# The floor of the sums of squares on VectorE, and GpSimd's root in three pieces with two operations between them

## The reference

```
xn   = layernorm(x)
q, k = l2norm(xn Wq^T), l2norm(xn Wk^T)   # per head, 16 heads of 16; l2norm(t) = t / max(|t|, 1e-6)
v    = xn Wv^T
s    = softmax(q k^T + alibi, window of 128 keys ahead) v, then Wo
h    = silu(fp4(xn) fp4(w_gate)^T) * (fp4(xn) fp4(w_up)^T)
g    = silu(fp4(h) fp4(w_down)^T)
out  = x + s * g
```

## Time and profile before

| | us |
|---|---|
| median of 3 runs | 504.02 (503.54 to 504.03) |
| the profiled execution's own time | 502.66 |
| its span | 500.7 |
| POOL busy | 412.1 (82%), 929 instructions |
| DVE busy | 432.3 (86%), 865 instructions |
| PE busy | 451.3 (90%) |
| ACT busy | 402.2 (80%) |

### The profile page before, as it was taken

How to read it: one execution, slowest core, us unless ns; L and a number is a source line. 1 busy time by engine, 2 the same in 40 slices (tenths; PEclk the granted TensorE clock), 3 DMA queues, 4 the chain that set the end, 5 groups by cost and what they waited for, 6 DMA issues and landing times.

```text
span 500.7 us, 14045 instructions
## 1 busy us (share of the span) xinstructions
PE 451.3 (90%) x4990; PEld 313.9 (63%) x4990; DVE 432.3 (86%) x865; ACT 402.2 (80%) x584; POOL 412.1 (82%) x929
## 2 busy tenths in 40 slices
PE   0467879999999999999999999999999999999997
PEld 0244556666666676676666677667666667666665
DVE  3989988889888888889988988888988888887686
ACT  1466988988888888888887888898888888888952
POOL 6554679999989989899988899989998998988751
PEclk9998999999999999999999999999999999999999
DMA  8211011222222112222221212222222111222200
GB/s 299 90 43 44 12 32 45 65 75 76 75 51 57 38 49 67 65 64 65 65 63 45 63 32 57 65 56 54 54 54 54 44 33 35 54 54 54 45 22 33
DMA packets 78277, 29.35 MB, mean 59 GB/s; under 512 B 67713, under 2 KB 77697, under 8 KB 78209
## 3 DMA queue, kind: packets, MB, share of 16 engines
q1 hardware_dynamic: 77920, 28.39, 22.3%
q10 hardware_dynamic: 288, 0.08, 0.1%
HBM read 7.49 MB, written 4.19 MB: 23 GB/s over the span
## 4 chain that ended last, share of the span: by engine, by line
POOL 56%; issue 17%; PE 5%; DVE 4%; ACT 3%; POOLq 1%; DVEq 0%; ACTq 0%
POOL probs L1514 12%; POOL probs L1507 7%; POOL y L1550 3%; POOL h_q L1544 3%; POOL xq L1526 3%; POOL xn L1604 3%; POOL ss L1562 2%; POOL h_scale L1534 2%; POOL rsq L1582 2%; POOL newton L1586 2%; POOL rsq L1575 2%; POOL x_scale L1521 1%; POOL rsq L1588 1%; POOL newton L1580 1%; POOL newton L1592 1%
## 5 line engine op out<-in xcount | busy, mean ns | idle before, releaser
L1322 ACT ACTIVATE probs<-scores 128x1024 f32<-128x1024 f32 (+1 forms) x101 | 102.3, 1013 | 2.6 <-PE scores L502 1.6
L1507 POOL TENSOR_SCALAR_AFFINE_SELECT probs<-probs 128x512 f32<-128x512 f32 x128 | 81.3, 637 | 1.7 <-ACT probs L1322 1.3
L1514 POOL TENSOR_SCALAR_AFFINE_SELECT probs<-probs 128x512 f32<-128x512 f32 x120 | 76.1, 636 | 3.7
L1200 ACT ACTIVATE qk_stack<-bank_q 128x512 f16<-128x512 f32 x64 | 35.1, 596 | 31.9 <-DVE bank_q L910 31.9
L595 PE MATMUL bank_b<-probs,vals 128*32 128x128 f32 x1952 | 59.7, 274 | 1.1 <-DVE vals L931 0.9
L595 PEld LDWEIGHTS bank_b<-probs,vals 128*32 128x32 f32 x1952 | 52.1, 110 | 7.9 <-DVE vals L931 7.0
L351 PE MATMUL gt<-wgu_hi,xT_hi 128*128 128x352 f16 x128 | 40.3, 315 | 12.1 <-ACT ffn_gate L1336 11.1
L784 DVE SCALAR_TENSOR_TENSOR xT_lo<-gt,xT_hi 128x512 f16<-128x512 f32 (+1 forms) x34 | 22.3, 657 | 27.6 <-ACT xT_hi L1200 27.6
L548 PE MATMUL gt<-wdn_hi,hT_hi 128*128 128x256 f16 x160 | 43.6, 273 | 0.6 <-DVE hT_lo L836 0.6
L548 PE MATMUL gt<-wdn_hi,hT_lo 128*128 128x256 f16 x160 | 43.6, 273 | 0.0
L548 PE MATMUL gt<-wdn_lo,hT_hi 128*128 128x256 f16 x160 | 43.6, 273 | 0.0
(11 more groups left out here) (219 smaller groups left out, 1456.5 us busy)
## 6 DMA issues: line engine op xcount, KB each, us to landing
out<-y SPq DMA_DIRECT2D x32, 128.0 KB, 2.0
x_all<-x SPq DMA_DIRECT2D x20, 128.0 KB, 2.1
x_all<-x SPq DMA_DIRECT2D x3, 512.0 KB, 4.2
x_all<-wproj SPq DMA_DIRECT2D x1, 768.0 KB, 7.1
dn_raw<-wd SPq DMA_DIRECT2D x1, 704.0 KB, 8.8
probs<-wg SPq DMA_DIRECT2D x1, 640.0 KB, 5.4
probs<-wu SPq DMA_DIRECT2D x1, 640.0 KB, 7.6
qk_slots<-qk_stack SPq DMA_TRANSPOSE x32, 3.7
```

Source lines behind the costliest of these rows:

```text
L1200: return e.activation(out, src, ACT.Copy, scale=up)
L1322: e.activation(probs[j % P_BUFS][:, grp, :, side(j), :], score_banks(j, grp)[:, :, :, side(j), :].rearrange("p b e h q -> p (b e) h q"), A ...
L1507: e.affine_select(out=own, in_=own, compare_op=ALU.is_ge, fill=0.0, base=0, pattern=[[0, GRP], [-1, P]], channel_multiplier=1).then_inc(s_ ...
L1514: e.affine_select(out=part, in_=part, compare_op=ALU.is_gt, fill=0.0, base=0, pattern=[[0, GRP], [1, P]], channel_multiplier=-1).then_inc( ...
```

## The change

The floor moves to DVE. There it is one more instruction behind `squares(t)`: directly behind `amax_x(t + 1)` in the loop, a few instructions behind `squares` in the other turns. GpSimd's `root` is cut into `root_seed` (SEED to LINEAR), `root_step` (QUAD to STEP) and `root_end` (Z_SQ to ROOT). In the loop `q_x(t)`, which stood behind the root, now stands between the first piece and the second, and `scale_x(t + 1)`, which stood two masks and an `x_norm` later, between the second and the third. Outside the loop the three pieces follow one another as before. The arithmetic is the same.

```
             def root(t):        # on VectorE, for tiles 0 and 1: as before
+            def floor_ss(t):    # now in the vector program
+                e.wait_ge(s_ss, t + 1)
+                e.tensor_scalar(ss[:, 0:2 * HEADS], ss[:, 0:2 * HEADS], (NORM_EPS * XW)**2, None, ALU.max).then_inc(s_floor, 1)
...
                 squares(t)
                 amax_x(t + 1)
+                floor_ss(t)
                 if exists(t + 3):
                     ln_stats(t + 3)
                 up_x(t)
...
             # GpSimd, the loop
                 mask_prev(t - 2, 3)
                 q_h(t - 3)
-                floor_ss(t)
-                root(t)
+                root_seed(t)
                 q_x(t)
+                root_step(t)
+                scale_x(t + 1)
+                root_end(t)
                 mask_own(t - 1, 0)
                 if exists(t + 2):
                     x_norm(t + 2)
                 mask_own(t - 1, 1)
-                scale_x(t + 1)
                 mask_prev(t - 1, 0)
```

More of the change, by code:

```diff
@@ L871, in squares, with floor_ss @@
                 e.tensor_reduce(ss[:, 0:2 * HEADS], qk_sq[:], AX, ALU.add).then_inc(s_ss, 1)
+            def floor_ss(t):
+                e.wait_ge(s_ss, t + 1)
+                e.tensor_scalar(ss[:, 0:2 * HEADS], ss[:, 0:2 * HEADS], (NORM_EPS * XW)**2, None, ALU.max).then_inc(s_floor, 1)
             def root(t):
@@ L1032, in vector_program @@
             squares(0)
+            floor_ss(0)
             scales_w(2)
@@ L1048, in vector_program @@
             values(0)
+            floor_ss(1)
             root(1)
@@ L1066, in vector_program @@
             values(2)
+            floor_ss(2)
             ln_stats(5)
@@ L1089, in vector_program @@
             hidden(1)
+            floor_ss(3)
             amax_h(1)
@@ L1145, in vector_program @@
             up_x(TILES - 1)
+            floor_ss(TILES - 1)
             grid_x(TILES - 1)
@@ L1558, in ln_parts, with root_seed @@
                 e.tensor_scalar(mean_col(t), moments[:, 0:1], -1.0, None, ALU.mult).then_inc(s_neg_mean, 1)
[L1560 to L1564, removed]
+            def root_seed(t):
                 y0, z, tmp, src = (w[:, root_cols(t)] for w in (rsq[0], rsq[1], newton, ss))
@@ L1582, in root, with root_step @@
                 e.tensor_scalar(z, tmp, -10.0 / 3.0, None, ALU.add).then_inc(s_rs, 1)
+            def root_step(t):
+                y0, z, tmp, src = (w[:, root_cols(t)] for w in (rsq[0], rsq[1], newton, ss))
                 e.wait_ge(s_rs, roots(t, LINEAR))
@@ L1588, in root, with root_end @@
                 e.tensor_tensor(z, tmp, y0, ALU.mult).then_inc(s_rs, 1)
+            def root_end(t):
+                y0, z, tmp, src = (w[:, root_cols(t)] for w in (rsq[0], rsq[1], newton, ss))
                 e.wait_ge(s_rs, roots(t, STEP))
@@ L1612, in gpsimd_program @@
             ln_parts(1)
-            root(-1)
+            root_seed(-1)
+            root_step(-1)
+            root_end(-1)
             x_norm(0)
@@ L1618, in gpsimd_program @@
             norm_w(3)
-            floor_ss(0)
             x_norm(1)
@@ L1630, in gpsimd_program @@
             ln_parts(3)
-            floor_ss(1)
             x_norm(3)
@@ L1638, in gpsimd_program @@
             q_x(1)
-            floor_ss(2)
-            root(2)
+            root_seed(2)
+            root_step(2)
+            root_end(2)
             mask_own(0, 3)
@@ L1654, in gpsimd_program @@
             scale_x(3)
-            floor_ss(3)
             ln_parts(5)
             mask_prev(1, 3)
-            root(3)
+            root_seed(3)
+            root_step(3)
+            root_end(3)
             mask_own(2, 0)
@@ L1691, in gpsimd_program @@
             q_h(TILES - 4)
-            floor_ss(TILES - 1)
-            root(TILES - 1)
+            root_seed(TILES - 1)
+            root_step(TILES - 1)
+            root_end(TILES - 1)
             mask_own(TILES - 2, 0)
```

## The result

| | before | after |
|---|---|---|
| median of 4 runs, us | 503.78 (502.77 to 504.03) | 512.36 (512.04 to 513.61) |
| ratio, 95% interval | 1 | 1.0182 (1.0169 to 1.0195) |
| the profiled execution's own time, us | 502.66 | 513.61 |
| its span, us | 500.7 | 511.9 |
| POOL busy, us | 412.1 | 406.9 |

The changed kernel is 1.8% slower: 9.2 us by the ratio, 8.6 by the medians. POOL is busy for 5.2 us less, DVE for 6.3 us more.

A forecast was written before the change was run, and what follows sets the result against it. POOL's 14.00 us row was taken to bound before, the loop through DVE and POOL after, at 14.35 a turn. Over 26 periods that gave +9.7, with the head's +0.2 making 504.02 + 9.9 = 513.9 us; range 504.0 to 518.5.

The forecast's parts named there:

- The bound moves from POOL to the loop: The way round `unit`, `h_grid`, `q_h`, root on DVE and POOL grows from 13.58 to 14.35 us, past POOL's own row.
- G: The end of `h_grid` on DVE, from which the prediction counts times in a turn; 7.69 us after `unit` starts.
- Crossings, 0.26: Root operations on POOL that start while DVE's `up_x` or `grid_x` runs end only after it: two crossings, 0.26 us.
- `q_x`, 0.48: `q_x` between LINEAR and QUAD on POOL adds 0.48 us to the way of the root; bounds 0.45 and 0.60.
- `scale_x`, 0.37: `scale_x` between STEP and Z_SQ on POOL hides no gap and adds 0.37 us; bounds 0.29 and 0.37.
- POOL's row of 13.35: POOL's own instructions per turn shrink from 14.00 to about 13.35 us, so POOL stands about a us at `q_h`.
- DVE's own 13.72: DVE's ordinary turn without its 0.28 us wait for the root, so at most 0.28 us a turn can be won.
- The head, +0.2: Before the loop, floors 0 to 2 add 0.20 us each on busy DVE, floor 3 relieves POOL: +0.2 us.
- full lockout: Rival: DVE's floor begins only behind `q_h`, SEED comes 0.15 later; 14.50 us a turn, 517.8 us; chance 0.08.
- The milder loss: Rival: the same loop without crossings, 14.09 us a turn, 507.2 us; chance 0.20.
- No change: Rival: inserts cost 0.6 instead of 0.85 and one crossing falls away; 13.95 to 14.03 a turn, about 504 us; chance 0.10.
- The faster case: Rival: POOL's freed 0.55 counts, the loop doesn't bind, DVE's 13.72 a turn sets the pace; 497.4 us; chance 0.12.

The follow-up runs named there:

- e6: The changed kernel with one more POOL operation each loop turn, a 256-column copy nobody reads: 513.04 us, ratio 1.0194 to the kernel before.
- e7: The kernel before with one more POOL operation each loop turn, a 256-column copy nobody reads: 519.34 us, ratio 1.0326.
- e1: The kernel before with only the floor moved to DVE, root in one piece, `q_x` and `scale_x` at their old places: 496.38 us, ratio 0.9897.
- e5: The changed kernel with no floor at all, SEED waiting for the sums of squares themselves: 513.06 us, ratio 1.0226 to the kernel before.
- e3: The changed kernel with `scale_x` back at its old place, only `q_x` inside the root: 501.65 us, ratio 0.9996 to the kernel before.
- e9: The kernel before with the floor and `scale_x` moved to DVE, two `x_scale` buffers, root in one piece: 492.15 us, ratio 0.9779.
- e2: The kernel before with only the new order on POOL, floor still on POOL: 514.07 us, ratio 1.0249.

## Why the prediction was right, and where it was not

The forecast said slower, 513.9 us, from a loop of 14.35 a turn; the chip gave 512.36 and 14.37. The mechanism is the one forecast. That the total comes out so close is in part luck, as the head and the total below show. Step by step:

- **The bound moves from POOL to the loop: right.** POOL waits for `h_grid` 29 times, the turn behind the batch's first tile lost its advantage, and e6 against e7 shows it without the model: a copy added on POOL costs nothing after, and 0.72 a turn before.
- **`unit` to G, 7.69: right,** the same number.
- **The floor: right.** Forecast: DVE's floor ends at G + 1.77 and SEED starts at G + 1.85. Measured: 255.13 (G + 1.76), 0.03 behind `h_q`'s end, and 255.22 (G + 1.85).
- **Crossings, 0.26: right** in size and place. Y_SQ took 0.36 and ARG 0.39, together 0.25 over their undisturbed 0.24 and 0.26. By the starts it is 0.30: SEED to the root's end is 3.96 in e1, against the 3.66 of the forecast. e5 shows that the size hangs on the place: one DVE operation earlier they are 0.39.
- **`q_x`, 0.48: right.** LINEAR's start to QUAD's start is 0.87 (256.45 to 257.32) and in e1 0.41 (249.25 to 249.66), so 0.46.
- **`scale_x`, 0.37: right.** STEP's start to Z_SQ's is 0.72 (258.06 to 258.78), and 0.34 in the earlier trace rows, so 0.38; e3 gives 0.40 by the periods.
- **Root end G + 6.62:** measured G + 6.65. Over 26 periods the loss is 10.06 where the sum had 9.7.
- **POOL's row of 13.35: wrong.** The sum took the floor off POOL at its full step of 0.55 and another 0.1 for lighter crossings. e1, where POOL doesn't wait in an ordinary turn, shows its row as 13.84: only 0.40 is saved up to SEED, and the root with its crossings gets longer by 0.22 instead of lighter. In the changed kernel it is about 14.37 - 0.64 = 13.73, since `h_q` without a wait starts 0.04 before its mask's end, as in e1. So POOL stands some 0.6 in a turn and not the 0.7 to 1.1 that the forecast named. The time didn't hang on it, since the loop of 14.35 is longer in either case.
- **DVE's own 13.72, and the 0.28 at most to be won: wrong.** e9, in which the root holds DVE up nowhere in an ordinary turn, runs at 13.61 on another loop, 0.39 below 14.00. The wait written beside `unit` counts from the end of the instruction before it, while an instruction that isn't held up starts 0.08 to 0.09 before that end (249.49 + 0.17 against 249.58 in e9). A wait of 0.28 is therefore about 0.37 of lost time.
- **The head, +0.2: a root was left out of the count.** Between the two profiles it was +1.07. Of this 0.65 is a miscount: 27 roots are interleaved and 26 periods were counted; the root of turn 4 lies in front of the unit step at which the count begins. There the way from `h_q`'s start to the root's end grew from 5.90 to 6.55. The other 0.4 lies in turns 0 to 3, and the change isn't what made it. PE ran there at the lower of its two clock levels (1.2 GHz) for part of the time, after it had stood still at 40 us: in the changed kernel from about 44 to 50.5 us, in the kernel before from about 45.5 to 48.5; the mean granted clock from 40 to 60 us is 0.83 and 0.91 of full speed. In e2, which has the head of the kernel before, and in e3, which has that of the changed kernel, it is 1.00 from 20 to 80 us. Their unit steps of tile 3 start at 70.78 and 70.84, against 71.74 and 72.15 in the two profiles. So the change costs turns 0 to 3 about 0.06, and the forecast's 0.2 was more than enough for them.
- **The total, +9.9: close, by luck.** Loop, turn 4 and head make 10.06 + 0.65 + 0.06 = 10.8, and yet the changed kernel's median lies only 8.6 above that of before. e6, which has the changed kernel's head and period, lies 10.3 above the kernel before on its own chip (513.04 against 502.71). The miss of 1.5 below 513.9 is thus in the base: the forecast added to the median of 504.02 and not to the profiled 502.66, from which it had 512.6. Why those first runs of before lay higher, no run shows.
- **The tail, nothing: right,** 37.08 and 37.15 from the last unit step to the end of the span.

The rivals: full lockout (14.50) falls with the floor's end at 0.03 behind `h_q`. The milder loss (14.09) falls with the crossings. No change falls with the insertions, 0.46 + 0.38 = 0.84 where it asked for 0.6. The faster case was wrong for the change, but its first half was worth more than nothing. Its argument, that POOL never waits and so the freed floor counts, is what e1 shows, with 0.16 a turn. What it lacked was the point at which the insertions eat this up, which e3 marks: `q_x` alone brings the period back to 13.97. The range was said to hold the forecast's own bounds; with both upper bounds at once (crossings 0.35, insertions 0.97) the loop is 14.56 and the time 519.4, just above 518.5.

## What to carry to other kernels

Where two engines wait for each other round a loop, the order on one of them can matter more than its load: an operation for which nobody waits belongs behind the result for which somebody does. Moved in front of it, it is paid in every turn as soon as that loop is the longest: here 0.46 for `q_x`, which is 0.62 long, and 0.38 for `scale_x`, which is 0.29 long. Before the load of the engine that never rests is lightened, the loop through it should be added up from the trace, since that sum says how much of the relief can be cashed and what comes next, which was a loop through ACT and PE here. And a small operation is best given to the engine whose next instruction waits for a third one, as `scale_x` in e9, where its 0.16 vanished in a wait of 0.75.

## What the runs showed of the hardware

- **A crossing costs a good part of the operation that is met, and a shift moves it.** A POOL mask went from 0.64 to 0.91 beside a DVE operation of 0.36 (e7); SEED from 0.22 to 0.46 beside one of 0.41 (e5). Taking the floor away made e5 slower than the changed kernel. In an experiment on this kernel that shifts one engine against the other, some 0.1 to 0.3 a turn may be this and not the edit.
- **A DVE operation with one input that meets a long POOL operation isn't held for a full length of its own behind it.** The floor on DVE took 0.32 and ended 0.03 behind `h_q`'s end; in e1 it took 0.63 (247.30 to 247.93) and again ended 0.03 behind (247.90). The Trainium skill (SBUF — State Buffer, Who interferes with whom) says that where VectorE works in a two-port mode, the later of the two is blocked completely while the other runs. The traces agree that it doesn't finish before POOL does; but if it began only then, it would end 0.17 later, the time that the floor takes in the changed kernel's tail (at 470.69), and it does not.
- **Small POOL operations keep a gap of 0.08 to 0.09 even where neither needs the other.** `scale_x` stands between two steps of the root and hides in neither gap: 258.06 + 0.26 to 258.40, and 258.40 + 0.29 to 258.78. Behind LINEAR and behind `h_q`'s first piece, in front of a larger operation, there is no gap: `q_x` starts at 256.74 where LINEAR ends at 256.78. Size alone doesn't decide it, though: e7's copy of 256 columns starts at 249.89, 0.08 behind the end of its mask (249.17 + 0.64).
